# Attention front of a Perceiver block: another order of exponentials, lag powers and lag products, and the last head's sum as identity products on TensorE

## What is computed

```python
Q = (x @ Wq).reshape(B, T, H, DH)              # B 4, T 128, H 4, DH 32
K = (ctx @ Wk).reshape(B, G, H, DH)            # G 2048, ctx has 384 columns
scores = einsum('bthd,bghd->bhtg', Q, K) / sqrt(DH), masked
# only the 32 largest scores of each row stay, then softmax;
# the mean over the 4 heads weighs the rows of ctx (4 x 128 x 384)
# S4D: dtA = dt * A, dC = C * (exp(dtA) - 1) / A
#      K[d, l] = 2 Re sum_n dC[d, n] * exp(dtA[d, n] * l),  l = 0..127, d = 0..511, n = 0..63
```

## Time and profile before

| | us |
|---|---|
| median of 3 runs | 874.61 (874.25 to 874.64) |
| the profiled execution | 877.79 |
| its span, first to last instruction | 876.0 |
| TensorE busy | 680.3 |
| VectorE busy | 387.5 |
| ScalarE busy | 262.0 |
| GpSimd busy | 222.3 |

### The profile page before, as it was taken

How to read it: one execution, slowest core, us unless ns; L and a number is a source line. 1 busy time by engine, 2 the same in 40 slices (tenths; PEclk the granted TensorE clock), 3 DMA queues, 4 the chain that set the end, 5 groups by cost and what they waited for, 6 DMA issues and landing times.

```text
span 876.0 us, 9936 instructions
## 1 busy us (share of the span) xinstructions
PE 680.3 (78%) x3780; PEld 312.1 (36%) x3780; DVE 387.5 (44%) x1204; ACT 262.0 (30%) x556; POOL 222.3 (25%) x137
## 2 busy tenths in 40 slices
PE   5856449738351988984999999977835999999997
PEld 2322125314231533432444444444332333333333
DVE  4947988968972504775100252036353111111104
ACT  2928689478761110000221001137110111001110
POOL 2493976848788100000000010000021000000003
PEclk9976678868585898997899999989957999999999
DMA  9850322404434393000002305000564699999934
GB/s 289 300 210 1 95 73 77 164 1 159 153 117 105 109 399 112 0 1 0 0 1 72 120 1 192 1 0 1 193 243 166 261 372 365 386 376 370 366 110 143
DMA packets 63553, 133.67 MB, mean 153 GB/s; under 512 B 8016, under 2 KB 18192, under 8 KB 62992
## 3 DMA queue, kind: packets, MB, share of 16 engines
q1 hardware_dynamic: 59104, 123.65, 39.1%
q0 software_dynamic: 1920, 6.29, 2.5%
q10 hardware_dynamic: 2480, 3.08, 1.1%
HBM read 122.59 MB, written 8.32 MB: 149 GB/s over the span
## 4 chain that ended last, share of the span: by engine, by line
PE 63%; DVE 14%; ACT 9%; DMA 7%; POOL 4%; issue 3%; SPq 1%; DVEq 0%; ACTq 0%; POOLq 0%
PE PS L1322 7%; PE PS L1458 6%; PE PS L1328 6%; PE PS L1476 6%; PE PS L1289 5%; PE PS L1126 4%; PE PS L1159 4%; PE PS L1482 3%; PE PS L1345 3%; PE PS L1463 3%; DMA AR<-in_ctxT 3%; PE PS L1202 3%; DVE AR L883 2%; PE PS L1176 2%; DMA token_rows<-AR 2%
## 5 line engine op out<-in xcount | busy, mean ns | idle before, releaser
L394 POOL TENSOR_TENSOR RS<-VE,CST 128x1 f32<-128x1 f32 (+2 forms) x19 | 12.2, 644 | 342.7 <-DVE VE L805 336.2
L1176 PE MATMUL PS<-AR,QT 32*128 32x512 f32 x128 | 45.3, 792 | 48.3 <-ACT AR L558 47.8
L1159 PE MATMUL PS<-AR,WK 128*128 128x512 f32 x96 | 53.7, 715 | 22.5 <-DMA AR<-in_ctxT 22.5
L1095 DVE COPY AR<-PS 128x512 f32<-128x512 f32 x10 | 6.8, 691 | 138.3 <-PE PS L1126 138.3
L842 DVE MAX8 KA<-AR 128x8 f32<-128x64 f32 x512 | 66.4, 212 | 1.3 <-issue 1.0
L1289 PE MATMUL PS<-AR,TT 128*128 128x512 f32 x128 | 60.0, 625 | 2.2 <-ACT TT L698 2.2
L1322 PE MATMUL PS<-TT,AR 128*128 128x512 f32 x128 | 57.5, 612 | 0.7 <-issue 0.7
L536 ACT ACTIVATE TT<-PS 128x512 f32<-128x512 f32 x12 | 7.2, 597 | 169.9 <-PE PS L1126 169.9
L525 POOL DMA_INDIRECT AR<-expert_rows,SLU x8 | 8.3, 1037 | 194.4 <-DMA expert_rows<-TT 192.2
L1476 PE MATMUL PS<-AR,TT 128*32 128x512 f32 x512 | 56.4, 592 | 0.8 <-issue 0.8
L1126 PE MATMUL PS<-CST,AR 128*128 128x128 f32 x152 | 25.4, 306 | 40.8 <-DMA AR<-token_rows 18.9
(11 more groups left out here) (275 smaller groups left out, 1202.7 us busy)
## 6 DMA issues: line engine op xcount, KB each, us to landing
AR<-in_w SPq DMA_DIRECT2D x32, 2048.0 KB, 12.5
AR<-in_ctxT SPq DMA_DIRECT2D x16, 768.0 KB, 8.4
AR<-in_ctx SPq DMA_DIRECT2D x16, 768.0 KB, 7.5
AR<-in_W SPq DMA_DIRECT2D x2, 4096.0 KB, 20.5
token_rows<-AR SPq DMA_DIRECT2D x1, 2560.0 KB, 15.0
AR<-token_rows SPq DMA_DIRECT2D x5, 512.0 KB, 6.8
X<-in_x SPq DMA_DIRECT2D x2, 1024.0 KB, 5.5
AR<-AR POOLq DMA_DIRECT2D x8, 256.0 KB, 3.8
```

The costliest lines, as they stand in the source:

```text
L1159: last = mm(PS[:, 4 + n % 2, :], WK[:, j, :], CXT[slot][:, j, :], start=j == 0, stop=j == KV - 1)
L1176: mm(PS[:, 2 * (k % 2) + j, :], QT[r, t], KT[b % 2][r, cols], start=True, stop=False)
```

## The change

On SyncE context chunks 4 and 5 are loaded ahead of the coefficients C_re and C_im and the small loads. On ScalarE exponentials(0) stands inside phase 0, ahead of the keys' last two chunks; powers(q) stands in the even phases, lag_turns and step_turns of group q + 1 in the odd ones before them; the copy of TM and the load of an activation table move. On VectorE whole(q) and diagonal(q) come two heads earlier, on GpSimd magnitudes, powers and fractions likewise. On TensorE lags(q) stands in the odd phase 2q + 1, ahead of context_rows(q - 1). The sum of head 15 leaves GpSimd: `last_rows` multiplies the 16 blocks of DS with the identity into banks 0 to 3 and accumulates the 16 blocks of W[1] times the identity onto them, so that the transposed sum of all four heads stands in PSUM. The reload of X waits for these products.

```diff
@@ SyncE
             for n in range(2, 4):
                 load_ctxT(n)
+            for n in (4, 5):
+                eng.wait_ge(S_["kt_ps"], n - 3)
+                load_ctxT(n)
             for n, a in ((2, "C_re"), (3, "C_im")):
...
-            for n in (4, 5):
-                eng.wait_ge(S_["kt_ps"], n - 3)
-                load_ctxT(n)
             eng.wait_ge(S_["zero"], 1)
...
-            eng.wait_ge(S_["added"], 3 * B)
+            eng.wait_ge(S_["at_ps"], 4 * B)
             load(X[:, :, :], I["x"].rearrange("b t d -> t b d"), "ld_x")
@@ GpSimd
                 b, h = divmod(i, XH)
-                if h == 0:
+                if h == 0 or i == NT - 1:
                     return
...
             coefficients()
+            magnitudes(0)
             for i in range(2, NT + 2):
                 q, k = divmod(i, 4)
-                if k == 0 and q:
-                    powers(q - 1)
+                if k == 0 and q < 4:
+                    fractions(q)
                 add_head(i - 2)
-                if k == 2 and 1 <= q < 4:
-                    fractions(q)
-                if k == 3 and q < 4:
+                if k == 1 and q < 4:
                     magnitudes(q)
+                if k == 2 and q < 4:
+                    powers(q)
@@ ScalarE
-                    eng.activation(AT[:, 4 * k:4 * k + 4, :], PS[:, 5 + k % 2, :]
+                    bank = 5 + k % 2 if b + 1 < B else k
+                    eng.activation(AT[:, 4 * k:4 * k + 4, :], PS[:, bank, :]
...
-            eng.wait_ge(S_["ld_small"], 16 * 5)
-            link(eng.activation(TM[:, :], TM8[:, :], ACT.Copy))
+            eng.preload_act_table_set("natural_log_exp_and_others")
             for m in range(NPH + 3):
                 q, late = divmod(m, 2)
-                if 1 <= m <= NPH:
+                if 2 <= m <= NPH:
                     exponentials(m - 1)
                 if late:
...
                         attended_rows(q - 1, (2, 3))
-                    if q < 4:
-                        powers(q)
+                    if q + 1 < 4:
+                        lag_turns(q + 1)
+                        step_turns(q + 1)
                 else:
                     for part in ((0, 1), (2, 3)):
                         if m + 1 < NPH:
                             scores(m + 1, part)
+                        if m == 0 and part[0]:
+                            exponentials(0)
                         if q + 1 < B:
                             context_keys(q + 1, part)
...
-                        eng.preload_act_table_set("natural_log_exp_and_others")
+                    if m == 2:
+                        eng.wait_ge(S_["ld_small"], 16 * 5)
+                        link(eng.activation(TM[:, :], TM8[:, :], ACT.Copy))
                     if q >= 2:
                         attended(q - 2)
-                    if 1 <= q < 4:
-                        lag_turns(q)
-                        step_turns(q)
+                    if q < 4:
+                        powers(q)
@@ VectorE
-                if k == 2 and 1 <= q < 4:
+                if k == 0 and 1 <= q < 4:
                     whole(q)
                 if 2 <= i < NT + 2:
                     masked(i - 2)
-                if k == 3 and q:
+                if k == 1 and q:
                     diagonal(q - 1)
@@ TensorE
+            def last_rows():
+
+                eng.wait_ge(S_["added"], 3 * B - 1)
+                eng.wait_ge(S_["s_sb"], 2 * GC * NPH)
+                for n in range(GT):
+                    mm(PS[:, n // 4, n % 4 * P:(n % 4 + 1) * P], DS[:, n * P:(n + 1) * P], ident, start=n % 4 == 0, stop=False)
+                eng.wait_ge(S_["masked"], NT)
+                for n in range(GT):
+                    last = mm(PS[:, n // 4, n % 4 * P:(n % 4 + 1) * P], W[1][:, n * P:(n + 1) * P], ident,
+                              start=False, stop=n % 4 == 3)
+                    if n % 4 == 3:
+                        last.then_inc(S_["at_ps"], 1)
...
                     if m + 1 < NPH:
                         scores(m + 1, (0, 1))
-                    if q:
+                    if 1 <= q < B:
                         attended_rows(q - 1, (0, 1))
                     if m + 1 < NPH:
                         scores(m + 1, (2, 3))
+                    if 1 <= q < B:
+                        attended_rows(q - 1, (2, 3))
+                    if q == B:
+                        last_rows()
+                    if q < 4:
+                        lags(q)
                     if q:
-                        attended_rows(q - 1, (2, 3))
                         context_rows(q - 1)
...
-                    if 1 <= q <= 4:
-                        lags(q - 1)
```

## The result

| | median us | ratio to before | 95% interval |
|---|---|---|---|
| before (runs beside it) | 874.0 | | |
| changed kernel | 876.52 | 1.0029 | 1.0015 to 1.0042 |

The change makes the kernel 2.5 us slower. The forecast was 7.1 slower: the sign was right, the size nearly three times too large. The spans of the two profiles (876.0 and 872.4 us) can't be compared as they stand: behind context_rows(3) both kernels have the same instructions, and the two executions differ there by 5.6 us (574.4 and 568.8). So I compare the attention stage, where the end of context_rows(3) moved from 301.61 to 293.01 + 10.59 = 303.60: +2.0, near the 2.5 of the medians. The other 0.5 us has no place that the profiles show.

A forecast was written before the change was run, and what follows sets the result against it. VectorE and ScalarE were taken to pace attention from the second pair, GpSimd its end, and TensorE everything after about 301 us. Terms +9.1 (front), +5.8 (legs between masks) and -7.8 (end) sum to +7.1: median 881.7 us, range 871 to 889.

The forecast's parts named there:

- The front: Attention stage up to mask 2: early exponentials(0) gains nothing, a new wait comes; mask 2 ends 9.1 us later.
- mask 2: VectorE's thresholding multiply for head 2; forecast to end at 108.5 us against 99.4.
- lag chain: GpSimd's coefficients(), magnitudes(0), powers(0), then lags(0) and both turns; forecast to hold mask 2, with exponentials done at 104.9 us.
- the early start: Mask 0 near 55 us instead of 70.30; kept, with a faster kernel, if GpSimd's powers(0) ends before 86.
- 2 to 4, 4 to 6, 8 to 10, 12 to 14: Changes in time between masks of those heads: +3.5, -0.3, -0.3 and -1.5 us.
- 6 to 8: Mask 6 to mask 8: late context chunk 1.6 us later, powers(2) +3.7, eased by 1.8; +3.5 us.
- the remainder: Unseen gain: clock high in context_rows(0) because lags(1) runs straight into it, late chunk earlier; chance 0.06.
- 10 to 12: Mask 10 to mask 12: +0.9 us, as the mask meets GpSimd's magnitudes(3).
- The end: Mask 14 to the end of context_rows(3): 27.35 us against 35.1, so -7.8; bounds -10 and -0.5.
- rival B: Clock stays low through last products and context_rows(3): tail gives 0.5 instead of 7.8, total +14.4, 889 us; chance 0.12.
- Rival A: Not slower: masks and GpSimd miss each other, 8.5 us less in all, 873.2; chance 0.24.
- Rival C: Late C_re and C_im loads start fractions(0) 5 us late and delay the chain: 886.7 us; chance 0.10.

The follow-up runs named there:

- e4: Changed kernel with exponentials(1) ahead of lag_turns(1), whole(1) one head later and fractions(1) behind the sum of head 2; ratio to before 1.0001.
- e9: e4 with the sum of head 1 straight behind coefficients() on GpSimd; ratio to before 0.9998.
- e6: Kernel before with exponentials(0) and its table load moved ahead, plus a GpSimd wait for the last queries; ratio 0.9897, median 869.41 us against 877.49.
- e1: Changed kernel with the sum of head 15 back on GpSimd and 16 transposes, new order kept; ratio to before 1.0041, median 878.43 us.
- e2: Kernel before with last_rows as its only change; ratio 0.9982 (0.9955 to 1.0009).
- e7: e6 with last_rows, the sum of head 14 ahead of powers(3), and lags(3) ahead of context_rows(3); ratio to before 0.9829, median 862.58 us.
- f2: Kernel before with 16 filler transposes of the identity ahead of each context_rows; ratio 0.9969.
- e10: Kernel before with the new order of the loads alone; ratio 0.9998.
- e3: Kernel before with exponentials(0) ahead of the last key chunks, its table load earlier, and magnitudes(0) ahead of the first head sum; ratio 1.0006.
- f1: Kernel before with 8 filler products of the identity with itself ahead of each context_rows; ratio 0.9976.
- e8: e7 with 16 filler transposes ahead of context_rows(0), (1) and (2); ratio to before 0.9864.

## Why the prediction was right and wrong

- **The front.** Right in place and order, and near in size: the early exponentials(0) is worth nothing in this order, the wait moves to whole(1), 15.6 us of it (I had some 15 to 17), mask 2 ends 7.6 later (I had 9.1). Three sizes were off: the masks cost coefficients() 3.0 us and not 4.1, and it began 0.3 earlier (end at 73.6, I had 75.0); powers(0) took 6.4 and not 7.35, since its first multiply took 1.96 and not 2.93; against this, mask 2 took 4.56 and not 3.6. What I missed is that the lag chain isn't the only holder: with it out of the way, the first head sum, which the change puts behind powers(0), still held mask 2 to 96.20 (e4), later than before. As it ends at 93.5 it cost nothing here. But the prediction says that the early start is kept if powers(0) ends before 86, and that leaves out this sum and the third wait (e9). What exponentials(0) is worth alone is the 8 us of e6.
- **2 to 4, 4 to 6, 8 to 10, 12 to 14.** Each is within 0.5 us.
- **6 to 8, the step that failed.** The prediction let the late context chunk come 1.6 us later against mask 6, since it kept context_rows(0) at its old 12.5 us and put 1.93 us of lags ahead of it. In the profile context_rows(0) took 10.59 us and lags(1) 1.45: with lags(1) in the place of the 0.69 us gap TensorE ran on from its transposes, the clock rose inside lags(1), and context_rows(0) had the high level from its first product. It ended 6.6 us ahead of mask 6's end instead of the forecast 4.3; from there the chunk took 13.1 us instead of 13.9, so it came 3.2 us earlier than forecast (170.81), and its key products took 6.91 instead of 7.75. These are 4.0 of the 4.3 us. This very gain stood in the prediction as the remainder, with 0.06 and no price, though it lies on the path through load_ctx(1).
  How much of it is the order's? Four kernels have lags(q) in that gap (the changed one, e1, e4, e9). Their context_rows(0) took 10.59, 10.59, 11.57 and 11.34 us, and their leg from mask 6 to mask 8 33.9, 34.5, 36.2 and 35.8 us, where the prediction had 38.2 and the kernel before 34.7. All twelve of their context_rows(0) to (2) lie between 10.6 and 11.9. So the price of 12.5 was wrong in each, by 0.9 to 1.9 us, and so was the leg, by 2.0 to 4.3. The full 4.3 is partly luck: where the clock rises differs from kernel to kernel, and the chunk's way (13.0 to 14.5 us) and its key products (6.9 to 8.5 us) vary over all profiles. Whether the closed gap counts or the longer stretch of work, the runs don't separate.
- **10 to 12.** The forecast +0.9 for mask 12 beside magnitudes(3) makes it 3.2 us; it took 5.08. GpSimd's two multiplies stand at 245.78 and 248.10. The mask began at 247.53; if its own 2.35 us came last, they began at 250.3, when the first multiply was over and the second nearly so. That is 1.8 of 2.4 us. The leg took 28.8 us in all four kernels with this order. Trainium skill, "SBUF — State Buffer", section "Who interferes with whom": the port pair that VectorE and GpSimd share is an exclusive lock. The trace agrees, and it looks as if a waiting instruction can lose it twice in a row.
- **The end.** It took 26.9 us against my 27.35: the products 5.1 and 3.7 (I had 6.2 and 4.2), context_rows(3) 10.59 at 1.00 (10.6), but 6.8 from mask 14 to the first product, with the last sum in it (I had 5.7). Right in sum; e1 and e2 say that the products are the small part of it. One bound was added up wrongly: all at 1.2 GHz makes 35.55 us, which is 0.5 more than the 35.1 before and not 0.5 less, so rival B should have stood at +15.4, near 890, outside the range.
- **The rule on transposes.** Trainium skill, "TensorE: Matmul & The Clock Gate", section "Part 4: PE-mode transpose", has them not count as busy for the clock in the same way, and the prediction says that the trace agreed. The 0.50 of the transposes from 284.4 to 288.4 was a stretch in which the clock had not yet come up, behind 7.46 us of waiting; products in such a stretch run at 0.50 too (the small ones of lags(3) from 275.13 took 1.93 us, against 1.10 in e7), so it says nothing on transposes. In f2 the clock rose while only transposes ran, and context_rows(0) took 10.49 us: for these float32 transposes the measurement goes against the rule. The 7.8 us of the tail did not need the rule.
- **Range and chances.** The time of 876.5 lies inside 871 to 889, and slower had 0.67. Rival A did not come: masks and GpSimd still met (masks 4 and 8 at 3.09 and 3.08 us, mask 12 at 5.08). Rival B did not: 1.00 in context_rows(3). Rival C is out by e10. The likeliest value was off by the front (1.5 us), by 6 to 8 (4.3) and, the other way, by 10 to 12 (2.4); the two legs had no bounds of their own, and 4.3 us is more than the 3 that the prediction allowed below for all six together. Had 10 to 12 been as forecast, the change would have cost almost nothing, so part of the right sign is luck.

## What to carry to other kernels

Pulling one step forward is worth only as much as the last of all the waits behind it allows: list every semaphore that the next step needs, buffers that another engine still reads among them, and not just the one that comes last today. Here three stood behind each other in the new order (lag chain, first head sum, powers(1)). In the old order none of them did: exponentials(0), moved ahead with only its table load, gave 1% (e6), and the rest of the new order gave it away. So try the smallest of the moves by itself first, and change nothing else with it; e3, with a second move in it, hid the gain. Ask of every product group what stood on TensorE just ahead of it: small work in a short gap can repay itself by the clock. And when a change has two parts, price the end of the stage for each alone and both ways round: the products gave 1.9 us behind the new order and 0.3 in the old one.

## What the runs showed of the hardware that I had not expected

- TensorE's clock rises during float32 transposes as during products: context_rows(0) took 12.46 us before, 10.49 behind filler transposes, 10.49 behind filler products.
- A gap of 0.69 us ahead of a product group went with a later rise of the clock: context_rows(0) to (2) took 12.0 to 13.6 us with it, 10.6 to 11.9 with 1.4 to 1.9 us of small products in its place, 10.5 with 2.4 to 2.9 us of filler. Where the clock was already up, the same gap cost nothing (context_rows(3) in the changed kernel: 10.59 at 1.00).
- Extra work that fills a gap made the kernel faster by 0.2 to 0.3% (f1, f2). On top of e7 it gave no gain in time (e8).
- A VectorE multiply with two inputs in SBUF took 5.08 us instead of 2.35 beside two GpSimd multiplies that followed each other.
